# The low parts of one expert's weights made on GpSimd instead of VectorE, and the last two output tiles of the kernel ended four steps apart

## What is computed

```
x = x + xattn(layernorm(x), ctx_1024, Wq, bq, Wk, bk, Wv, bv)
xn = layernorm(x)
probs = softmax(xn @ gate_w)                       # 4 x 1024 x 8
top_p, top_idx = top_k(probs per batch and expert, 256)
xin = xn[top_idx]                                  # 8 x 4 x 256 rows of 256
h = gelu(xin @ w1[e])                              # 1024 wide
y = (h @ w2[e]) * top_p
x = x + scatter_add(y at top_idx)
```

## Time and profile before

| | |
|---|---|
| median of 3 runs | 473.53 us |
| the profiled execution | 473.02 us, of which its span is 471.3 us |
| TensorE matmuls busy | 443.5 us, 94% of the span |
| VectorE busy | 318.1 us, 67% |
| ScalarE busy | 212.3 us, 45% |
| GpSimd busy | 204.7 us, 43% |
| TensorE on the chain that ended last | 79% of the span |
| mean granted TensorE clock | 0.958 of full speed |

### The profile page before, as it was taken

How to read it: one execution, slowest core, us unless ns; L and a number is a source line. 1 busy time by engine, 2 the same in 40 slices (tenths; PEclk the granted TensorE clock), 3 DMA queues, 4 the chain that set the end, 5 groups by cost and what they waited for, 6 DMA issues and landing times.

```text
span 471.3 us, 8224 instructions
## 1 busy us (share of the span) xinstructions
PE 443.5 (94%) x2586; PEld 374.6 (79%) x2586; DVE 318.1 (67%) x830; ACT 212.3 (45%) x524; POOL 204.7 (43%) x230
## 2 busy tenths in 40 slices
PE   8999455999999999999999999999999999999993
PEld 7877333887888888888888888888888888888993
DVE  4698989797676567656756675667566756674551
ACT  2488994224362445244524452454245424442331
POOL 6544503031835381538154814481448144813342
PEclk9999755799999999999999999999999999999997
DMA  8984862015428150815081408150815081504142
GB/s 275 362 293 163 295 278 105 23 48 184 79 53 224 36 80 23 223 38 76 23 223 41 72 23 223 44 74 19 223 46 74 17 223 46 79 12 46 15 49 30
DMA packets 35671, 52.51 MB, mean 111 GB/s; under 512 B 3009, under 2 KB 28994, under 8 KB 35138
## 3 DMA queue, kind: packets, MB, share of 16 engines
q1 hardware_dynamic: 22946, 34.89, 22.1%
q0 software_dynamic: 12288, 17.08, 21.2%
q10 hardware_dynamic: 416, 0.27, 0.2%
HBM read 35.17 MB, written 16.92 MB: 111 GB/s over the span
## 4 chain that ended last, share of the span: by engine, by line
PE 79%; DVE 2%; DMA 1%; POOLq 0%; POOL 0%; ACT 0%; issue 0%; ACTq 0%; DVEq 0%
PE bank L1054 36%; PE wide L1071 23%; PE wide L1075 12%; PE bank L821 3%; PE wide L1066 2%; PE bank L1029 1%; DMA xg<-xn_rows,gidx 1%; PE bank L1111 1%; PE wide L821 1%; DVE hlo L1516 0%; POOLq L92 0%; POOL out_dram L587 0%; DVE hhi L1514 0%; PE bank L1117 0%; DVE place L1705 0%
## 5 line engine op out<-in xcount | busy, mean ns | idle before, releaser
L1071 PE MATMUL wide<-w2both,hhi 128*128 128x512 f32 x480 | 176.2, 400 | 0.2 <-DVE ysb L1528 0.2
L587 POOL DMA_INDIRECT out_dram<-ysb,sidx x64 | 107.2, 1675 | 107.3 <-DVE ysb L1528 82.2
L759 ACT ACTIVATE hraw<-bank 128x512 f32<-128x512 f32 (+1 forms) x136 | 77.6, 571 | 137.4 <-PE bank L1054 135.8
L1075 PE MATMUL wide<-w2both,hlo 128*128 128x256 f32 x480 | 134.2, 280 | 0.0
L579 POOL DMA_INDIRECT xg<-xn_rows,gidx x64 | 67.8, 1059 | 129.7 <-issue 95.8
L1514 DVE CAST hhi<-hraw 128x512 fp32r<-128x512 f32 (+1 forms) x136 | 57.8, 425 | 75.5 <-ACT hraw L759 75.3
L1071 PEld LDWEIGHTS wide<-w2both,hhi 128*128 128x128 f32 x480 | 90.4, 188 | 20.1 <-DVE hlo L1516 0.6
L1516 DVE TENSOR_TENSOR hlo<-hraw,hhi 128x512 fp32r<-128x512 f32 (+1 forms) x136 | 90.0, 661 | 4.7
L1075 PEld LDWEIGHTS wide<-w2both,hlo 128*128 128x128 f32 x480 | 90.3, 188 | 3.5
L1054 PE MATMUL bank<-xlo,w1hi 128*128 128x512 f32 (+1 forms) x268 | 80.4, 381 | 0.0
L1054 PE MATMUL bank<-xhi,w1lo 128*128 128x512 f32 (+1 forms) x268 | 80.2, 380 | 0.0
(11 more groups left out here) (198 smaller groups left out, 434.4 us busy)
## 6 DMA issues: line engine op xcount, KB each, us to landing
raw<-in_w_dram SPq DMA_DIRECT2D x16, 1024.0 KB, 6.9
xn_rows<-x_all SPq DMA_DIRECT2D x4, 1060.0 KB, 4.2
x_all<-in_x_dram SPq DMA_DIRECT2D x8, 512.0 KB, 10.1
raw<-in_x_turned_dram SPq DMA_DIRECT2D x8, 512.0 KB, 9.2
out_dram<-x_all SPq DMA_DIRECT2D x8, 512.0 KB, 4.8
xg<-xn_rows,gidx POOLq DMA_INDIRECT x64, 2.9
out_dram<-ysb,sidx POOLq DMA_INDIRECT x64, 4.2
ctxT<-in_ctx_turned_dram ACTq DMA_DIRECT2D x1, 256.0 KB, 3.6
```

Of the source, the lines that this page charges most:

```text
L587: pool.indirect_dma_start(out=out_rows, out_offset=at, in_=ysb[g][:, i, :], in_offset=None, compute_op=ALU.add).then_inc(rows_added, 16)
L759: act.activation(hraw[s % 2][:, 0:width], bank[s % 2][:, 0:width], ACT.Gelu).then_inc(gelu_done, 1)
L1071: return pe.matmul(y[:, 0:2 * C], hhi[s % 4][:, at], w2both[:, j].rearrange("p a d -> p (a d)"), start=(j == 0), stop=(j == HC - 1), skip_ ...
L1075: return pe.matmul(y[:, 0:C], hlo[s % 4][:, at], w2hi[:, j, :], start=False, stop=False, skip_group_check=True)
```

## The change

For the first expert alone, the sixteen subtractions move from VectorE's queue to GpSimd's: the eight of w1 ahead of gather 0, the eight of w2 between gather 0 and gather 1. For the other experts nothing moves. In the tail a fifth buffer of half width holds the last step's `hhi` and `hlo`, `last_rows` covers five steps instead of four, and the last two tiles end four tile-steps apart instead of two.

```diff
-        hhi = [sb(f"hhi{i}", [P, UT], F32R) for i in range(4)]
-        hlo = [sb(f"hlo{i}", [P, UT], F32R) for i in range(4)]
+        hhi = [sb(f"hhi{i}", [P, UT if i < 4 else UT // 2], F32R) for i in range(5)]
+        hlo = [sb(f"hlo{i}", [P, UT if i < 4 else UT // 2], F32R) for i in range(5)]
...
+        def h_at(s, last):
+
+            return 4 if last and s == steps_of(last) - 1 else s % 4
...
-            for g in range(NU):
-                pool.wait_ge(xn_stored[g], 16 * HB)
-                pool.wait_ge(gidx_ready, g + 1)
-                gather(g, FIRST if g == 0 else 0)
+            pool.wait_ge(own_set, 2 + 2 * B + 3 * HB)
+            for j in range(HC):
+                pool.wait_ge(w1_hi, j + 1)
+                pool.tensor_tensor(w1lo[:, j], w1raw[:, :, bass.ts(j, P)], w1hi[:, j].bitcast(F32),
+                                   ALU.subtract).then_inc(w1_split, 1)
+            pool.wait_ge(xn_stored[0], 16 * HB)
+            pool.wait_ge(gidx_ready, 1)
+            gather(0, FIRST)
+            for j in range(HC):
+                pool.wait_ge(w2_hi, j + 1)
+                pool.tensor_tensor(w2lo[:, j], w2raw[:, j], w2hi[:, j].bitcast(F32), ALU.subtract).then_inc(w2_split, 1)
+            pool.wait_ge(xn_stored[1], 16 * HB)
+            pool.wait_ge(gidx_ready, 2)
+            gather(1)
...
-            TAIL = 4
+            TAIL = 5
 
             def last_rows(e, steps):
-                a, b, c, z = range(steps - TAIL, steps)
-                ff1(c, ST * e + c, e, True)
-                ff1(z, ST * e + z, e, True)
-                for s in (a, b, c):
+                o, a, b, c, z = range(steps - TAIL, steps)
+                for s in (b, c, z):
+                    ff1(s, ST * e + s, e, True)
+                for s in (o, a, b, c):
                     pe.wait_ge(h_split, ST * e + s + 1)
                     ff2_tile(s, NL - 2, e, True)
-                for s in (a, b):
-                    ff2_tile(s, NL - 1, e, True)
+                ff2_tile(o, NL - 1, e, True)
                 pe.wait_ge(h_split, ST * e + z + 1)
                 ff2_tile(z, NL - 2, e, True).then_inc(tile_done, 1)
-                for s in (c, z):
+                for s in (a, b, c, z):
                     t = ff2_tile(s, NL - 1, e, True)
                 t.then_inc(tile_done, 1)
...
-            w1_rest(0, 0)
             keep_reached(1, 5)
-            w1_rest(1, 1)
             candidates(1, 6)
...
-            for j in range(3):
-                w2_rest(j, j)
             keep_reached(1, 8)
-            w1_rest(6, 6)
...
-            for j in range(3, 7):
-                w2_rest(j, j)
...
-                    if s == 0:
+                    if s == 0 and not is_first(e):
                         w2_rest(HC - 1, HC * e + HC - 1)
```

More of the change, by code:

```diff
@@ L1065, in ff2_tile @@
                     for m, (hh, w) in enumerate(((hhi, w2hi), (hhi, w2lo), (hlo, w2hi))):
-                        t = pe.matmul(y[:, 0:C], hh[s % 4][:, at], w[:, j, :], start=(j == 0 and m == 0),
+                        t = pe.matmul(y[:, 0:C], hh[h_at(s, last)][:, at], w[:, j, :], start=(j == 0 and m == 0),
                                       stop=(j == HC - 1 and m == 2), skip_group_check=True)
@@ L1070, in by_hi @@
                 def by_hi():
-                    return pe.matmul(y[:, 0:2 * C], hhi[s % 4][:, at], w2both[:, j].rearrange("p a d -> p (a d)"),
+                    return pe.matmul(y[:, 0:2 * C], hhi[h_at(s, last)][:, at], w2both[:, j].rearrange("p a d -> p (a d)"),
                                      start=(j == 0), stop=(j == HC - 1), skip_group_check=True)
                 def by_lo():
-                    return pe.matmul(y[:, 0:C], hlo[s % 4][:, at], w2hi[:, j, :], start=False, stop=False,
+                    return pe.matmul(y[:, 0:C], hlo[h_at(s, last)][:, at], w2hi[:, j, :], start=False, stop=False,
                                      skip_group_check=True)
@@ L1513, in split_h @@
                 dve.wait_ge(gelu_done, n + 1)
-                dve.tensor_copy(hhi[s % 4][:, 0:width], hraw[s % 2][:, 0:width]).then_inc(h_hi, 1)
+                dve.tensor_copy(hhi[h_at(s, last)][:, 0:width], hraw[s % 2][:, 0:width]).then_inc(h_hi, 1)
                 dve.wait_ge(h_hi, n + 1)
-                dve.tensor_tensor(hlo[s % 4][:, 0:width], hraw[s % 2][:, 0:width],
-                                  hhi[s % 4][:, 0:width].bitcast(F32), ALU.subtract).then_inc(h_split, 1)
+                dve.tensor_tensor(hlo[h_at(s, last)][:, 0:width], hraw[s % 2][:, 0:width],
+                                  hhi[h_at(s, last)][:, 0:width].bitcast(F32), ALU.subtract).then_inc(h_split, 1)
             def w2_rest(j, n):
@@ L1635, in _ @@
             compare(1, 1, 6)
-            w1_rest(2, 2)
             keep_reached(1, 6)
-            w1_rest(3, 3)
             candidates(1, 7)
@@ L1641, in _ @@
             compare(1, 1, 7)
-            w1_rest(4, 4)
             keep_reached(1, 7)
-            w1_rest(5, 5)
             candidates(1, 8)
@@ L1666, in _ @@
             compare(1, 1, 9)
-            w1_rest(7, 7)
             keep_reached(1, 9)
```

## The result

| | before | changed |
|---|---|---|
| median of 7 runs, taken in turn on one chip | 473.58 us | 479.73 us |
| ratio, with its 95% interval | | 1.0109 (1.0081 to 1.0136) |
| profiled execution | 473.02 us | 479.36 us |
| its span | 471.3 us | 477.6 us |
| mean granted TensorE clock | 0.958 | 0.951 |

The changed kernel is slower, by 1.1% or 5.2 us (3.8 to 6.4 us); 475.4 us was forecast and the range ended at 477.2 us. Some executions are several per cent longer at a lower granted clock (505.83 us for one of the changed kernel), and all ratios leave them out, while the medians, here 6.2 us apart, do not. Its span is 6.3 us longer than before, at the upper end of the interval.

A forecast was written before the change was run, and what follows sets the result against it. Time lost before the first gather was taken as time of the kernel, with VectorE's queue the path up to the list. +3.2 - 0.5 - 0.8 = +1.9 us gave 475.4 us on the median; range 472.2 to 477.2 us.

The forecast's parts named there:

- the main term: Ahead of the first gather: GpSimd and VectorE take turns at SBUF, making list and queue ready 3.2 us late.
- Part 1: Sixteen subtractions off VectorE: second list 1.2 us sooner, 0.1 us from the third split, 0.4 from ScalarE's wait; -0.5 us together.
- Part 2, ahead of the gather: Eight w1 subtractions on GpSimd, 0.7 us each, take turns with VectorE's 14 two-operand instructions; list 3.2 us late.
- Rival (a): Ahead of the gather: no taking of turns for arithmetic, gather at most 0.1 us late; 472.3 us, chance 0.20.
- rival (b): Ahead of the gather: only part of GpSimd's time excludes VectorE, delay 0.4 to 2.2 us; about 473.9 us, chance 0.15.
- rival (c): Ahead of the gather: GpSimd is slow, 1.0 us or more a piece, +5.6 us delay; 477.8 us, chance 0.11.
- Part 2, behind the gather: Eight w2 pieces on GpSimd after gather 0, VectorE's operands mostly in PSUM: cost 0, at worst +0.5 us.
- The tenth comparison may wait once: Behind gather 0: one VectorE comparison waits for GpSimd's w2 pieces by some 0.3 us, costed at 0.
- at most one instruction: Ahead of the gather: VectorE and GpSimd take turns, each waiting for the other's one instruction in front, 0.7 us a piece.
- Part 3: Tail: two more tile-steps of 0.355 us let the last scatter issues start 0.7 us sooner; -0.8 us, between -0.3 and -0.9.
- The sum: Whole kernel: +3.2 - 0.5 - 0.8 = +1.9 us on the profiled 473.02 us, giving 474.9 us.

The follow-up runs named there:

- the swapped kernel: The change with seven w2 pieces ahead of gather 0, the eight of w1 behind it and the last of w2 last; ratio 1.0144 to the kernel before.
- the run with writes only: The kernel before plus sixteen 128 x 256 GpSimd fills of an unused buffer where the change's w1 pieces stood; 474.94 us in the profiled execution.

## Why the prediction was wrong

The sign and the mechanism of the main term held; the size did not: +1.9 us was forecast, +5.2 us measured. The span of the changed kernel is 6.3 us longer; from the timelines it divides like this. "Gather" is the start of its first issue, "step" the first `ff1` of the third step, "clock" the time from the gather to the rise of TensorE's granted clock, all in us. "Spaced" is the change with gaps between the w2 pieces, "held" the one in which they wait for the comparison.

| | gather | gather to step | step to end of span | span | clock |
|---|---|---|---|---|---|
| before | 78.09 | 12.14 | 381.07 | 471.3 | 9.2 |
| changed | 81.01 | 14.65 | 381.94 | 477.6 | 8.6 |
| changed, w2 spaced | 80.89 | 12.13 | 379.98 | 473.0 | 8.9 |
| changed, w2 held | 81.28 | 11.36 | 380.06 | 472.7 | 7.2 |
| w1 alone on GpSimd | 81.67 | 11.14 | 381.29 | 474.1 | 7.1 |
| w2 on GpSimd, new tail | 78.53 | 11.67 | 380.00 | 470.2 | 7.9 |

**Part 1** (-0.5 us, of which 0.4 ScalarE's wait). ScalarE's wait of 1.07 us is 0.17 us in the changed kernel:

```profile
120.77 0.42 ACT L753 ACTIVATE w1hi<-raw 128x256 fp32r<-128x256 f32 x1 [0.17 <-DMA raw<-in_w_dram]
```

From step to end the held and the spaced kernel have 1.0 and 1.1 us less than before, 0.7 of it the tail's, so 0.3 to 0.4 us is left for this. Nearly right. The w1 subtractions were put at 0, and no run shows otherwise. Gather to step is indeed 0.8 to 1.0 us shorter in the held kernel and in that with w1 alone; but in both TensorE's clock rose 2 us sooner behind the gather than before, and 2 us less at half clock are worth up to 1.0 us. With w2 spaced, all sixteen are off VectorE too, the clock rose about as late as before, and gather to step is what it was before; with w1 on VectorE and the clock's rise at 7.9 us it is 0.5 us shorter. The gain goes with the clock's rise, not with the place of the subtractions.

**Part 2, ahead of the gather** (list 3.2 us late; measured 2.8). One piece takes 0.73 us, 0.7 was taken. The estimate of 0.75 us worked out from the Trainium skill (GPSIMD Engine Reference, "Performance versus the Vector engine") lies within 0.02 us of that. The way the 3.2 us were put together was half wrong: I let each engine wait for the other and both be late, all 14 two-operand instructions and eight pieces one after the other. GpSimd hardly waited: two pieces of 0.87 us, some 0.3 us in all (eight pieces take 5.84 us here, 5.50 in the swapped kernel, where they shut VectorE out). VectorE did nearly all the waiting, in six rows of 0.3 to 0.6 us, and only for as long as the pieces ran; the other two-operand instructions came behind them at their old lengths. With half the pieces the delay was 1.1 us. Rival (a), no taking of turns, is excluded by the stretched rows, rival (b) by the 2.8 us, and rival (c) by the 0.73 us.

**Part 2, behind the gather: here the prediction failed.** Its step was "The tenth comparison may wait once, by some 0.3 us ... I cost it at 0, at worst +0.5 us". The one that waited was the second comparison of the ninth round, which the prediction had taken to be over by then, and it waited not for one piece but for seven, 5.05 us. The ninth pair begins 4.5 us behind the gather's start, before and now. But GpSimd's second and third issue, 1.17 and 1.16 us before, take 0.95 and 1.06 us now that no subtraction of VectorE runs beside them, and so the last issue ends 5.1 us behind the gather's start instead of 5.4 us. Before, the pair was over 0.2 us ahead of that end; now its second comparison was still under way.

In the table the cost is changed against spaced, whose gather and clock's rise lie within 0.3 us of the changed kernel's: gather to step is 2.5 us longer and step to end 2.0 us, together 4.5 us; against held it is 3.3 and 1.9 us, together 5.2 us. Of this 2.16 us are TensorE's stop. The rest, 2.3 to 3.0 us, goes with the clock: TensorE ran at half of it from 93 to nearly 100 us (the stretch table has 0.50 there, 1.00 in the held kernel), some 2.6 us of that ahead of the step and 4.2 us behind it. In the medians changed differs from spaced and held by 3.9 and 4.5 us, by the ratios by about 3 us.

I had carried over from the front of the gather the rule "at most one instruction", and I had looked only at whether VectorE's operands in that stretch lie in PSUM "mostly"; the comparison's do not, and a count on TensorE hangs on it.

The Trainium skill (SBUF — State Buffer, "Who interferes with whom") says that the engine that loses the shared access stays blocked until the other's instruction is through. The trace agrees for pieces with a gap between them and for instructions that begin in the midst of the pieces: 0.3 to 0.6 us each ahead of the gather, 1.0 us for the comparison of the spaced kernel. It does not for the comparison that was under way when GpSimd went from a DMA issue into its pieces; there the measurement decides, and it was blocked for the whole row of seven. That fillings do not stretch two-operand instructions, which the same section states, the run with writes only confirms.

**Part 3** (-0.8 us; measured -0.7). The scales are 1.42 us apart as worked out, and the second issue is bound by the first.

**The sum**, redone in the profile's numbers: +2.9 (gather later) + 2.5 (gather to step: the stop, and half clock behind it) + 2.0 (half clock behind the step, against the spaced kernel) - 1.1 (second list and tail, as in the spaced kernel) = +6.3 us. Without the shutting out the spaced kernel has +1.7 us in its span and the held one +1.4 us, 2.4 and 2.2 us by their ratios, and +1.9 had been forecast. That it fits so well is partly luck: ahead of the gather 0.4 us too much was taken, and for the second list and the tail 0.2 to 0.3 us too much gain.

**What stays open.** Why a comparison that has begun is shut out over all seven pieces, and not only over one, is not shown. It is in both traces of the change (5.44 us each) and in that of the swapped kernel, each time with GpSimd coming straight out of a DMA issue. With GpSimd idle before, it did not happen. The first of the w1 pieces (71.82 us) began inside a comparison, 0.14 us before its end, and gapless pieces followed; the comparison kept its 0.38 us. So it is in every kernel with w1 on GpSimd. The eighth w2 piece began inside the split of `hlo`, and there GpSimd waited. That speaks for the DMA issue in front as part of the cause, but the overlaps differ in place and length, and no run took the issue away and left the rest.

## What to carry to other kernels

Work moved to an idle engine is not free if it reads SBUF beside VectorE instructions with two SBUF operands: count those on the path, and let each cost up to one of the other engine's instructions, here 2.8 us for eight pieces. A row of such instructions without gaps, directly behind a DMA issue, is a risk of another size, the length of the row, for a two-operand VectorE instruction that is under way when it begins; place it where the critical VectorE instruction is over, and hold it there with a wait. Ask also what the freed engine's neighbours now do sooner: here 0.3 us less in the issues made the two meet. And when TensorE stops in a stretch in which its clock is just rising, price the stop with what comes behind it: here a stop of 2.2 us went with 2.3 to 3.0 us more lost at half clock. Last, before a gain is given to a moved instruction, compare where the clock rose.

## What the runs showed of the hardware that was not expected

- One VectorE instruction of 0.38 us took 5.44 us beside seven gapless GpSimd instructions, and the pair 6.44 us beside eight; with a completion wait between the pieces the pair took 1.67 us. In all of these GpSimd came straight from a DMA issue; with GpSimd idle before its first piece, a comparison under way kept its 0.38 us.
- The contention is uneven for arithmetic: the eight GpSimd pieces took 5.82 to 5.86 us in every kernel that had them ahead of the gather, against 5.50 us in the swapped kernel, while a VectorE scan went from 0.21 to 0.74 us. But GpSimd waits too: pieces of 0.73 us took 0.87 to 1.05 us where they met VectorE's longer instructions. DMA issues on GpSimd became longer beside two-operand instructions of VectorE: 1.0 us to 1.32 and 1.75 us.
- GpSimd's fills left two-operand instructions alone and stretched small one-operand ones on integers, 0.17 to 0.35 us. In the swapped kernel such a one (`block_of`) took 0.65 us beside a piece of w2.
- TensorE's granted clock, full from 90 us on, went back to half at 93 us, after a stop of 2.16 us that ended at 91.27 us, and stayed there until nearly 100 us although TensorE was 4.75 of 5.00 us busy from 94 to 99 us; in the held and the spaced kernel, without the stop, it stayed full.
- TensorE's clock rose between 7.1 and 9.9 us behind the start of the gather in these kernels, and gather to step, where nothing was shut out, between 11.14 us and 12.22 us, the shortest with the earliest rise and the longest with the latest.
